# Attention by chunks of 128 tokens: scores in four row groups, values padded to 128 columns, the diagonal queries made by ScalarE, and the order of four engines' work arranged anew

## The reference, cut to what matters

```python
q = (x @ W_q.T).reshape(b, t, h, dh)      # k and v likewise
decay = jnp.where(diff >= 0, gammas[:, None, None] ** pow_, 0.0)
attn = jnp.einsum('bihd,bjhd->bhij', q, k) * decay[None] / scale
y = jnp.einsum('bhij,bjhd->bihd', attn, v)
# ... y is normalised per sequence and head, scaled, shifted, and multiplied by W_o
```

## Time and profile before

| | |
|---|---|
| median of 3 runs | 1013.8 us |
| lowest and highest | 1006.59 and 1016.2 us |
| the profiled execution | 1016.33 us |
| its span, first to last instruction | 1014.4 us |
| mean granted TensorE clock | 0.895 |
| PE busy | 951.6 us (94%) |
| DVE busy | 721.5 us (71%) |
| ACT busy | 581.3 us (57%) |
| POOL busy | 418.8 us (41%) |
| share of PE on the chain of waits | 89% |

### The profile page before, as it was taken

The page is one execution under the profiler, slowest core; times in us unless marked ns, Lnnn a source line. Parts: engine busy times, 40 slices in busy tenths (PEclk is TensorE's granted clock), DMA queues, the critical chain, the costliest instruction groups (busy, mean ns, idle before and its releaser), DMA issues.

```text
span 1014.4 us, 21372 instructions
## 1 busy us (share of the span) xinstructions
PE 951.6 (94%) x6656; PEld 896.7 (88%) x6656; DVE 721.5 (71%) x1195; ACT 581.3 (57%) x1009; POOL 418.8 (41%) x369
## 2 busy tenths in 40 slices
PE   4869999999999999999989999999999999999864
PEld 2349999999999999999989999999999999999854
DVE  6777766676667767666777777777777777777576
ACT  4623433343334434334768888777888888777641
POOL 3135655555445645553123333333333333333245
PEclk9967977797778978777899999999999999999978
DMA  9932222222222322226456666676666666765577
GB/s 310 342 84 79 75 73 68 62 73 72 68 68 74 78 68 74 72 60 235 171 196 225 223 228 221 225 242 237 246 228 223 226 222 226 236 243 195 176 240 257
DMA packets 106248, 170.47 MB, mean 168 GB/s; under 512 B 30768, under 2 KB 77232, under 8 KB 96240
## 3 DMA queue, kind: packets, MB, share of 16 engines
q1 hardware_dynamic: 99408, 151.49, 46.0%
q0 software_dynamic: 6816, 18.69, 5.1%
HBM read 115.88 MB, written 33.18 MB: 147 GB/s over the span
## 4 chain that ended last, share of the span: by engine, by line
PE 89%; DVE 5%; DMA 3%; issue 1%; POOL 1%; SPq 1%; ACT 0%; POOLq 0%; DVEq 0%; ACTq 0%
PE ps L683 35%; PE ps L875 22%; PE ps L790 13%; PE ps L739 7%; PE ps L747 3%; PE ps L860 2%; DMA arena_f<-pair_rows 2%; PE ps L756 2%; PE ps L814 1%; PE ps L701 1%; DMA xn<-x 1%; PE ps L730 1%; PE ps L693 1%; DVE arena_f L1306 1%; DVE arena_f L961 1%
## 5 line engine op out<-in xcount | busy, mean ns | idle before, releaser
L683 PE MATMUL ps<-arena_r 128*128 128x256 f32 (+2 forms) x2640 | 391.3, 305 | 0.9 <-DVE arena_f L1144 0.9
L683 PEld LDWEIGHTS ps<-arena_r 128*128 128x128 f32 x2640 | 356.4, 197 | 15.7 <-issue 1.5
L875 PE MATMUL ps<-arena_r 128*128 128x256 f32 x1872 | 233.9, 285 | 0.8 <-DVE gn_t L1275 0.8
L875 PEld LDWEIGHTS ps<-arena_r 128*128 128x128 f32 x1872 | 230.2, 194 | 0.9 <-issue 0.9
L479 POOL TENSOR_TENSOR fence_out<-eps_col 128x1 f32<-128x1 f32 x39 | 77.7, 1991 | 310.9 <-DVE arena_f L1206 310.9
L539 ACT ACTIVATE arena_r<-arena_f 128x2048 fp32r<-128x2048 f32 x78 | 145.6, 1923 | 0.2 <-issue 0.2
L790 PE MATMUL ps<-arena_r 128*128 128x32 f32 x1024 | 141.8, 287 | 0.0
L790 PEld LDWEIGHTS ps<-arena_r 128*128 128x128 f32 x1024 | 140.3, 223 | 0.0
L458 POOL TENSOR_TENSOR arena_r<-arena_f,arena_r 128x512 fp32r<-128x512 f32 x64 | 94.4, 1481 | 86.6 <-ACT arena_r L546 84.9
L617 ACT ACTIVATE arena_f<-ps,arena_f 128x256 f32<-128x256 f32 x156 | 65.5, 472 | 90.7 <-PE ps L875 85.5
L1222 DVE TENSOR_TENSOR arena_r<-arena_f,arena_r 128x2048 fp32r<-128x2048 f32 x39 | 89.4, 2292 | 34.9 <-ACT arena_r L539 34.9
(11 more groups left out here) (138 smaller groups left out, 1022.3 us busy)
## 6 DMA issues: line engine op xcount, KB each, us to landing
arena_f<-w SPq DMA_DIRECT2D x78, 1024.0 KB, 5.0
xs_rows<-spare_rows SPq DMA_DIRECT2D x39, 258.0 KB, 3.6
arena_f<-xs_rows SPq DMA_DIRECT2D x39, 258.0 KB, 2.6
arena_r<-arena_r SPq DMA_DIRECT2D x256, 32.0 KB, 2.0
pair_chunk<-xn SPq DMA_DIRECT2D x32, 256.0 KB, 2.6
arena_f<-pair_rows SPq DMA_DIRECT2D x16, 512.0 KB, 5.3
arena_f<-b SPq DMA_DIRECT2D x39, 128.0 KB, 2.9
xn<-x SPq DMA_DIRECT2D x8, 512.0 KB, 8.6
```

The source lines that it names most:

```text
L683: last = pe.matmul(out_ap, lhs(a), rhs(b), start=start and n == 0, stop=stop and n == 2, **kw)
L875: last = pe.matmul(ps[:, 2 + hp, o * SLOT:(o + 1) * SLOT], w1_r[par][:, a, at:at + P], xs_r[:, b, k * SLOT:(k + 1) * SLOT], start=(m == 0 ...
```

## The change

- **Scores.** Chunk n's scores are made of 24 matmuls of 32 contracted rows by 256 columns, where there were 12 of 128 rows by 512 columns. Group g of the four uses the partitions 32g to 32g+31 of keys and queries (two heads in each half of the 256 model columns) and writes its own PSUM bank; the four groups follow one another for each half and pass. The heads in a bank are others than before, so `inside` reads them from other places. The signals of the four banks come with the last four matmuls.
- **Diagonal queries.** `q_diag` has 256 columns a half, and two ACT instructions for each chunk fill it: each is a copy of all query parts (4x128 a partition) with a scale per partition of 1 or 0 (`own_head`). The eight DMAs of a chunk and two memsets go, and a memset of the wide values comes.
- **Values.** `v_wide` holds four heads in 4x128 columns, each head's 32 value columns in the place that they have in the output and zeros beside them. `inside` has 32 matmuls as before, each with 128 moving columns in place of 32, and each adds to the four heads' 128 output columns.
- **Across.** For each half one matmul takes the high queries by the high and low state together (256 columns), and one the low queries by the high state (128), where there were three of 128.
- **Order.** The lists of PE, DVE, ACT and POOL are arranged anew; `projections`, `keys_and_queries` and `new_state` are split in two. DVE's masking waits for its own low parts in two more places, and `act.wait_ge(across_done, NT)` and `dve.wait_ge(u_psum, NT)` guard the room of the first experts' second weights.

```diff
...
+        "own_head": (local[:, None] % QH == np.arange(QH)[None, :]) * 1.0,
...
         xt = fr(2, 2, KC * P)
+        v_wide = fr(2, NB, HB * P)
+        diag_at = fr.at
+        q_diag = fr(2, 2, KC, QH * P)
+        fr.at = diag_at + 2 * KC * F
+        kq_t = fr(2, 2, 2, KC * P)
         k_r = fr(2, 2, D)
-        v_r = fr(2, H, 2, DH)
-        kq_t = fr(2, 2, 2, KC * P)
-        diag_at = fr.at
-        q_diag = fr(2, 2, KC, HP * P)
+        fr.at = diag_at + 4 * KC * F
         s_r = fr(2, 2, NB, HB * P)
         state_r = fr(2, KC * P)
+        def v_part(par, part, g0=0, groups=NB):
+            return bass.AP(v_wide.tensor, v_wide[:, par, g0, part * DH:part * DH + 1].offset,
+                           [list(v_wide.ap[0]), [HB * P, groups], [P + 2 * DH, HB], [1, DH]])
+
...
-            def queries_to_diagonal(n, par):
-
-                wait(sp, s["s_psum"], NB * (n - 1))
-                sp.wait_ge(s["kqt_h"], n + 1)
-                sp.wait_ge(s["kqt_l"], n + 1)
-                for h in range(HP):
-                    r = slice(h * DH, (h + 1) * DH)
-                    sp.dma_start(q_diag[r, par, :, :, h * P:(h + 1) * P].bitcast(F32).rearrange("p s c i -> p (s c) i"),
-                                 kq_t[r, par, 1].bitcast(F32).rearrange("p s (c i) -> p (s c) i", c=KC)).then_inc(s[f"q_diag{par}"], 16)
...
-            for par in range(2):
-                nc.gpsimd.memset(q_diag[:, par].bitcast(F32), 0.0).then_inc(s["r_zero"], 1)
+            nc.gpsimd.memset(v_wide.bitcast(F32), 0.0).then_inc(s["r_zero"], 1)
...
+                    act.wait_ge(s["kqt_l"], n + 1)
+
+                    wait(act, s["s_psum"], NB * (n - 1))
+                    for o in range(QH):
+                        nc.scalar.activation(q_diag[:, np_, :, :, o * P:(o + 1) * P], kq_t[:, np_, 1].rearrange("p s (c i) -> p s c i", c=KC),
+                                             ACT.Copy, scale=C["own_head"][:, o:o + 1]).then_inc(s["q_diag"], 1)
...
+                    nc.scalar.activation(v_part(np_, 0), v_f[:, np_].rearrange("p (g h d) -> p g h d", g=NB, h=HB), ACT.Copy).then_inc(s["v_h"], 1)
...
+            act.wait_ge(s["across_done"], NT)
             w_high(1, 0, 0)
             xs_high(0, 0)
...
-                pe.wait_ge(s[f"q_diag{par}"], (n - par) * 64 + 128)
-                for g in range(NB):
-
-                    wait(pe, s["s_f"], NB * (n - 1) + g + 1 if not isinstance(n, int) or n > 0 else 0)
-                    c, col = g // 2, g % 2 * HB * P
-                    parts(ps[:, g, :], lambda a: kq_t[:, par, 0, a, c * P:(c + 1) * P],
-                          lambda b: q_diag[:, par, b, c, col:col + HB * P], True, True).then_inc(s["s_psum"], 1)
+                pe.wait_ge(s["q_diag"], QH * (n + 1))
+                for c in range(KC):
+                    for m, (a, b) in enumerate(PASSES):
+                        for g in range(NB):
+                            rows = slice(g * QR, (g + 1) * QR)
+                            if c == 0 and m == 0:
+
+                                wait(pe, s["s_f"], NB * (n - 1) + g + 1 if not isinstance(n, int) or n > 0 else 0)
+                            last = pe.matmul(ps[:, g, c * QH * P:(c + 1) * QH * P], kq_t[rows, par, 0, a, c * P:(c + 1) * P],
+                                             q_diag[rows, par, b, c], start=(m == 0), stop=(m == 2))
+                            if c == KC - 1 and m == 2:
+                                last.then_inc(s["s_psum"], 1)
...
                 y_bank = ps[:, 7, :].rearrange("p (h s d) -> p h s d", h=H, s=2)
                 for c in range(KC):
-                    last = parts(y_bank[:, c * HP:(c + 1) * HP, 0], lambda a: kq_t[:, par, 1, a, c * P:(c + 1) * P],
-                                 lambda b: state_r[:, b, c * P:(c + 1) * P], c == 0, False, skip_group_check=True)
+                    heads = y_bank[:, c * HP:(c + 1) * HP]
+                    both = state_r[:, :, c * P:(c + 1) * P].rearrange("p s (h d) -> p h s d", h=HP)
+                    pe.matmul(heads, kq_t[:, par, 1, 0, c * P:(c + 1) * P], both, start=(c == 0), stop=False, skip_group_check=True)
+                    last = pe.matmul(heads[:, :, 0], kq_t[:, par, 1, 1, c * P:(c + 1) * P], state_r[:, 0, c * P:(c + 1) * P],
+                                     start=False, stop=False, skip_group_check=True)
                 last.then_inc(s["across_done"], 1)
...
                 for h in range(H):
+                    g, col = h % HP // QH, (h // HP * QH + h % QH) * P
                     for a in range(2):
-                        last = pe.matmul(ps[:, 7, h * 2 * DH:(h + 1) * 2 * DH],
-                                         s_r[:, par, a, h // HB, h % HB * P:(h % HB + 1) * P],
-                                         v_r[:, par, h].rearrange("p s d -> p (s d)"), start=False,
+                        last = pe.matmul(ps[:, 7, h // HB * P:(h // HB + 1) * P],
+                                         s_r[:, par, a, g, col:col + P],
+                                         v_wide[:, par, h // HB, h % HB * P:(h % HB + 1) * P], start=False,
                                          stop=(h == H - 1 and a == 1), skip_group_check=True)
...
-                                 lambda b: v_r[:, par, c * HP:(c + 1) * HP, b], c == 0, c == KC - 1, skip_group_check=True)
+                                 lambda b: v_part(par, b, c * HP // HB, HP // HB), c == 0, c == KC - 1, skip_group_check=True)
...
             def chunk(i, par):
+                if within(i, NT):
+                    scores(i, par)
+                if within(i - 1, NT):
+                    state_sums(i - 1, 1 - par)
                 if within(i + 1, NT):
                     kq_transposes(i + 1, 1 - par)
-                if within(i, NT):
-                    scores(i, par)
                 if within(i + 2, NT):
                     x_transposes(i + 2, par)
                 if within(i - 1, NT):
-                    state_sums(i - 1, 1 - par)
                     inside(i - 1, 1 - par)
+                if within(i + 2, NT):
+                    key_value_projection(i + 2, par)
+                if within(i + 2, NT):
+                    query_projection(i + 2, par)
                 if within(i - 2, NT):
                     y_transposes(i - 2, par)
-                if within(i + 2, NT):
-                    projections(i + 2, par)
                 if within(i, NT):
                     across(i, par)
...
+            dve.wait_ge(s["u_psum"], NT)
...
```

More of the change, by code:

```diff
@@ L42 @@
 NB = H // HB
+QH = 2
+QR = QH * DH
 E, F = 8, 1024
@@ L549, in chunk @@
                 n, np_ = i + 1, 1 - par
+                if within(i, NT):
+                    score_high(i, par, 0)
                 if within(n, NT):
@@ L1174, in _ @@
             second_expert()
-            keys_and_queries(0, 0)
+            keys(0, 0)
+            queries(0, 0)
             slots_of_experts()
@@ L1181, in _ @@
             values_low(0, 0)
-            keys_and_queries(1, 1)
+            keys(1, 1)
+            queries(1, 1)
             experts_of_slots()
```

115 lines of the change are left out of this document (64 added, 51 removed).

## The result

The changed kernel takes **879.18 us** (median of 4 runs, 877.28 to 888.77); the kernel before took 1010.19 us beside it (4 runs, 997.41 to 1016.2). The ratio is 0.8793, 95% interval 0.8665 to 0.8921. The profiled execution had 879.42 us, a span of 877.6. All ratios in this document leave out runs that were slow at a lower granted clock; of low_parts_apart, the last experiment, that leaves two of four (982.15 and 989.43 us), and its rows are of the run of 997.9 us.

A forecast was written before the change was run, and what follows sets the result against it. The prediction took PE's attention work, at a lowered clock, as the bound. It took 28 x (13.02 - 9.6) = 96 us, plus 4 and 9 at the ends, 109 in all, off 1016.3 for 907 us; range 890 to 955.

The forecast's parts named there:

- What bounds it: Attention: PE's chain of nine pieces, 10.85 us a chunk at full clock, 13.02 measured; the lower clock costs 2.17.
- The padding: `inside`, 32 to 128 columns: 3.45 us a chunk, free as work, and the clock stays up.
- The scores: 24 pairs in four row groups: 1.44 us a chunk, between 0.72 side by side and 2.88 one after another.
- two drains of under 0.5 us: Tiling changes around the scores drain PE: below 0.5 us a chunk, held inside the scores' range.
- PE's sum: PE's pieces of one chunk at full clock: 9.21 us in all, 8.49 to 10.65 with the scores' bounds.
- DVE at 8.7 us: DVE's unchanged work per chunk, nearly as full as PE; so 9.6 us a chunk, 0.4 over PE's sum for waits.
- The ends: Outside the 28 chunks: 4 us saved in the first two chunks, 9 between the last `across` and the experts.
- The diagonal queries and the order: ACT's two added instructions hidden at 6.4 to 7.0 us a chunk; SP's eight dropped DMAs a chunk counted at nothing.
- 1: Scores: the row groups' weight loads run one after another; chunk 10.8 us, 943 us in all; chance 0.18.
- 2: DVE or its order becomes the bound, some 10.8 us a chunk, again about 943 us; chance 0.12.
- 3: The clock still falls, in `inside` or the scores, about as often as before: 966 us; chance 0.08.
- 4: Slower: without the long full-row scores PE enters `inside` at a low clock and stays low; about 1150 us; chance 0.04.

The follow-up runs named there:

- low_parts_apart: dve_tail_old with one wait added: POOL's second low part of scores starts only when DVE's first is done; 993.66 us, ratio 0.9879.
- groups_in_turn: Changed kernel with the scores' loops exchanged, all six pairs of one row group before the next group; 920.32 us, ratio 0.92.
- diag_by_dma: Changed kernel with the diagonal queries laid out by eight SP DMAs a chunk in place of ACT's two instructions; 1028.43 us, ratio 1.0365.
- dve_tail_old: Changed kernel with DVE's list alone back to nearly the order of before, keys and queries last; 1001.59 us, ratio 0.9952.
- old_order_dma: Changed kernel with all four lists in the order of before and the diagonal queries by eight SP DMAs a chunk; 961.8 us, ratio 0.9558.
- pe_order_old: Changed kernel with PE's list alone in the order of before; 916.73 us, ratio 0.912.
- old_order: Changed kernel with the lists of PE, ACT, DVE and POOL in the order of before; 933.99 us, ratio 0.9393.
- narrow32: Changed kernel with `inside` moving 32 columns a matmul again; 934.37 us, ratio 0.9341.

## Why the prediction was right or wrong

**What bounds it: right.** PE's work at its granted clock before, PE's work at full clock now; the chain holds nothing else.

**The padding: right,** price and effect. 3.45 us taken, 3.52 measured; 1.00 in place of 0.80.

**The scores: mis-sized, the largest miss.** 1.44 us taken as a middle between bounds of 0.72 and 2.88, measured 0.91: 28 x 0.53 = 15 us. The place between full overlap and a limit by issue was chosen by a row of tiny matmuls (0.085 each), which is no floor for groups that overlap: 0.91/24 is 0.038. The estimate from the Trainium skill's clock gate page (Part 3), 0.94, was the better one, and I had set it aside. That two drains of under 0.5 us lie inside the range was right, but I left them out of the sum: the state sums are 0.20 longer.

**PE's sum:** 9.21 taken, 8.73 measured. Scores -0.53, state sums +0.20, transposes -0.23 (0.90 for 1.13; those of keys and queries take 0.46 behind the state sums, 0.62 in their old place), inside and projections +0.12, `across` -0.04.

**DVE at 8.7 us and "0.4 over PE's sum for waits that two full engines give each other": wrong.** DVE has 7.5 us a chunk. I had read its work as durations, and those held time in which DVE and POOL stop one another: 0.97 for 0.70 and 0.92 for 0.56 on DVE, 1.48 for 1.29 on POOL. The new order lays them apart for the most part. So DVE was no second full engine, the allowance was for nothing (28 x 0.39 = 11 us), and it was this that held the range's lower end at 9.1 us a chunk, although PE's own lower bound was 8.49.

**The ends: about right** (2.4 and 11.2 us against 4 and 9). With 3.4 us in the unchanged rest the account closes: 907 - 14.8 (scores) + 1.4 (the rest of PE's sum) - 10.9 (allowance) - 0.6 (ends) - 3.4 = 878.7, against 879.4 profiled.

**The diagonal queries and the order: costed at nothing, which holds only for all parts together.** ACT's work is 161.91/250 x 8.74 = 5.7 us a chunk and hidden. But I called the move from SP to ACT free in both directions ("PE never waited"): without it the new order makes 1028 us. And I treated the order as a risk of the change, where it carries some 55 of the 131 us once the other parts are in. Row groups and ACT's copies without it move the end by 1%.

**The rivals.** 1 fell by groups_in_turn: even serial groups would cost 920, not 943. 2 is false of the new order, for which it was reckoned; a bound of its kind shows in the old one (934). 3 fell: the clock holds. 4, slower by the clock, did not come by the way I named, PE entering `inside` low: it comes by waits of PE for others, as diag_by_dma shows at 1028.

## What to carry to other kernels

When a change shortens the engine that bounds, the order in which the others do their work becomes part of the change: cost the ring from its result back to its next input, not the busy sum of each engine, and count every issue of a queue in it. A duration read where two engines lie side by side is not the price of the work; look for the same shape elsewhere in the trace before it becomes a floor. And a wait of TensorE can cost several times its length, if the clock falls behind it: in diag_by_dma one of 2.2 to 3.2 us came once in two chunks, and two chunks took 27.0 us in place of 17.5.

## What the runs showed of the hardware

- The clock fell in two ways. Without any idle time of PE, with series of 128x32 and 128x64 matmuls (0.83 and 0.84 in the attention); with 128x128 in the same place it held. And behind idle times of PE, with 128 columns: behind all 14 of 2.2 to 3.2 us in diag_by_dma, behind nine of 19 of 1.7 to 2.3 us in dve_tail_old, 11 of 17 of 1.3 to 1.8 us in low_parts_apart, six of 12 of 1.0 to 2.2 us in old_order_dma, and none of 28 of 1.0 to 1.1 us in pe_order_old. So the length of one idle time does not tell alone whether a fall follows.
- Between the last chunk and the experts the clock was at half for 23.9 us in old_order and groups_in_turn and for 27.3 us in narrow32, and at full speed throughout in the changed kernel. Why was not tried.
- A load and matmul of 32 rows by 256 columns, one behind another in the same rows, costs 0.081 us (with the way into the row groups in it), one of 128 rows 0.120. What part of it is the load is not settled.
- The first scores' piece is 0.18 us longer than a repeated one, and the full-row matmuls behind the row groups are 0.15 to 0.20 us longer (0.37 for 0.22 and 0.82 for 0.62): up to 0.38 us together for going in and out.
- DVE operations that read and write SBUF alone are held up by POOL's of the same kind, up to 1.65 us for 0.69, and POOL's a little by them (1.29 to 1.48). The masks, which read PSUM, are not (0.68 in every kernel). Where exactly one lets the other go was not tried.
